# Norms of the queries as rows in a gated cross-attention and local-attention kernel on Trainium2

## The reference, cut to what matters

```python
l2norm = lambda t: t / jnp.maximum(jnp.linalg.norm(t, axis=-1, keepdims=True), 1e-12)
q, k = l2norm(q) * qs, l2norm(k) * ksc
q = q * cos * scale + rotate_half(q) * sin * scale
k = k * cos * inv + rotate_half(k) * sin * inv
sim = jnp.einsum('bhwie,bhwje->bhwij', bq, bk2) * QK_SCALE
sim = jnp.where(mask, -jnp.finfo(sim.dtype).max, sim)
attn = jax.nn.softmax(sim, -1)
out = jnp.einsum('bhwij,bhwje->bhwie', attn, bv2)
```

## Time and profile before

| | |
|---|---|
| Median of 3 runs | 1986.11 us (1985.73 to 1987.9) |
| The profiled execution, own time | 1993.02 us |
| its span, first to last instruction | 1991.2 us |
| TensorE busy | 1858.3 us (93%) |
| VectorE busy | 1589.7 us (80%) |
| ScalarE busy | 1045.7 us (53%) |
| GpSimd busy | 903.9 us (45%) |
| mean granted TensorE clock | 0.970 |

### The profile page before, as it was taken

The page is one execution under the profiler, slowest core; times in us unless marked ns, Lnnn a source line. Parts: engine busy times, 40 slices in busy tenths (PEclk is TensorE's granted clock), DMA queues, the critical chain, the costliest instruction groups (busy, mean ns, idle before and its releaser), DMA issues.

```text
span 1991.2 us, 84866 instructions
## 1 busy us (share of the span) xinstructions
PE 1858.3 (93%) x35408; PEld 1303.1 (65%) x35408; DVE 1589.7 (80%) x3092; ACT 1045.7 (53%) x1879; POOL 903.9 (45%) x1231
## 2 busy tenths in 40 slices
PE   6888858899999999999999999999999999999996
PEld 3444424676767777777767677776767676777674
DVE  5565557788988888888888888888889888888883
ACT  2444423455555656555555556565556555465553
POOL 1000015364554646464555546464645555464640
PEclk7898888999999999999999999999999999999997
DMA  2001006556566656566565666565665646564650
GB/s 69 10 7 64 0 3 100 83 80 102 74 122 109 94 82 94 117 95 108 78 104 72 122 109 94 82 93 117 93 110 76 106 71 124 104 95 83 91 91 22
DMA packets 73332, 166.87 MB, mean 84 GB/s; under 512 B 16592, under 2 KB 23504, under 8 KB 72400
## 3 DMA queue, kind: packets, MB, share of 16 engines
q0 software_dynamic: 36864, 100.71, 37.9%
q1 hardware_dynamic: 36432, 65.68, 12.7%
HBM read 20.57 MB, written 1.05 MB: 11 GB/s over the span
## 4 chain that ended last, share of the span: by engine, by line
PE 69%; DVE 9%; issue 7%; DMA 2%; ACT 0%; DVEq 0%; POOL 0%; POOLq 0%; ACTq 0%
PE ps L997 14%; PE ps L1033 8%; PE ps L1087 7%; PE ps L1107 6%; PE ps L1057 6%; PE ps L1141 5%; PE ps L1009 5%; PE ps L1070 4%; PE ps L1100 3%; DVE big L815 3%; PE ps L1131 3%; PE ps L1021 3%; DVE big L825 2%; DMA big<-big 2%; PE ps L1048 2%
## 5 line engine op out<-in xcount | busy, mean ns | idle before, releaser
L477 POOL DMA_DIRECT2D big<-big x768 | 607.0, 1497 | 62.4 <-DVE big L807 43.9
L564 ACT ACTIVATE big<-ps 128x512 f32<-128x512 f32 x384 | 228.4, 595 | 587.6 <-PE ps L997 540.0
L997 PE MATMUL ps<-big,wn_sb 128*128 128x256 f32 x1536 | 411.2, 396 | 17.5 <-issue 14.9
L815 DVE TENSOR_TENSOR big<-big,ps 128x512 f32<-128x512 f32 x384 | 249.6, 680 | 93.2 <-PE ps L1021 82.8
L997 PEld LDWEIGHTS ps<-big,wn_sb 128*128 128x128 f32 x1536 | 275.4, 192 | 69.6 <-issue 16.5
L468 POOL TENSOR_TENSOR big<-big 128x512 f32<-128x512 f32 x96 | 123.4, 1285 | 360.8 <-ACT big L581 360.8
L804 DVE TENSOR_TENSOR big<-ps,tab 128x512 f32<-128x512 f32 x384 | 262.0, 682 | 11.0 <-ACT big L564 10.9
L807 DVE TENSOR_TENSOR big<-ps,tab 128x512 f32<-128x512 f32 x384 | 259.0, 674 | 0.0
L1141 PE MATMUL ps<-big,wo_sb 128*128 128x256 f32 x768 | 214.5, 382 | 0.0
L443 POOL COPY big<-xs 64x256 f32 x144 | 79.2, 550 | 263.5 <-DVE xs L843 257.6
L1033 PE MATMUL ps<-wn_sb,big 128*64 128x512 f32 x768 | 182.0, 611 | 0.7 <-DVE big L807 0.7
(11 more groups left out here) (146 smaller groups left out, 2917.1 us busy)
## 6 DMA issues: line engine op xcount, KB each, us to landing
big<-big POOLq DMA_DIRECT2D x768, 128.0 KB, 5.0
big<-big SPq DMA_DIRECT2D x96, 256.0 KB
big<-big SPq DMA_DIRECT2D x96, 192.0 KB
wn_sb<-in_wn SPq DMA_DIRECT2D x6, 1024.0 KB, 10.0
wn_sb<-in_wn SPq DMA_DIRECT2D x6, 512.0 KB, 6.1
wo_sb<-in_wo SPq DMA_DIRECT2D x6, 512.0 KB, 4.0
w_sb<-in_w SPq DMA_DIRECT2D x6, 341.0 KB, 3.0
w_sb<-in_w SPq DMA_DIRECT2D x6, 192.0 KB, 3.3
```

The source lines that it names most:

```text
L477: eng.dma_start(rot[to:to + 32, at:at + 4, :], src[32 * r:32 * r + 32], accum_op=ALU.add).then_inc(added[i], 16)
L564: eng.activation(sq[:, two, :], ps[:, i % 2, :].rearrange("p (a t) -> p a t", a=2), ACT.Square).then_inc(sq_d, 1)
L815: eng.tensor_tensor(hat[:, two, :], rot[:, two, :], ps[:, i % 2, :].rearrange("p (a t) -> p a t", a=2), ALU.mult).then_inc(hat_d, 1)
L997: mm = eng.matmul(ps[:, k % 2, a * T:a * T + T], wn_sb[:, u * P:u * P + P], sT, start=True, stop=True)
```

## The change

The queries are no longer normalized ahead of the scores. `rot` holds them as they are (with the factor 256 of the spreads put into the rotary tables), and the scores read queries from `rot` and keys from `hat`, which is half as large. The queries' reciprocal norms, made for all heads in n_r, are turned by two transposes (Q0, `turn_norms`) so that tokens lie on partitions, copied to SBUF by ScalarE (q0), and a new VectorE step M multiplies them into the scores on their way out of PSUM into `pr_`. X and D then work on `pr_` in SBUF. R and H are left for the keys alone, four each. Since `rot` is read by the scores, c0 and c4 of the next round wait for S0 and S1; S1 and the weighing steps wait for M where they waited for D. The four plans are new. N3 to N6 stay as they are. POOL_PLAN is unchanged.

```diff
@@ -57,7 +57,7 @@
 ...
     other = np.arange(P) ^ 32
-    rot = np.stack([8.0 * both(cq), 8.0 * both(sq)[other], both(ck), both(sk)[other]], 1).astype(f)
+    rot = np.stack([2048.0 * both(cq), 2048.0 * both(sq)[other], both(ck), both(sk)[other]], 1).astype(f)
     q, k = np.arange(WIN)[:, None], np.arange(KW)[None, :]
@@ -180,7 +180,7 @@
 ...
         rot = view(UNITS * T, UNITS, T)
-        hat = view(UNITS * T, UNITS, T)
+        hat = view(PAIRS * T, PAIRS, T)
         pr_ = view(2 * 2 * 512, 2, 8, 2 * KW)
@@ -203,6 +203,7 @@
 ...
         top = sb("top", [P, 2, 2, 8])
+        rq = sb("rq", [P, NT, P])
         den = sb("den", [P, 2, 2 * 8])
@@ -237,6 +238,7 @@
 ...
                    "wo_d", "x_d", "w_go", "s_go", "vf_free", "y2_d", "den_h", "den_s"))
+        rq_t, rq_d, mul_d = sem("rq_t"), sem("rq_d"), sem("mul_d")
         chain, nchain, nmid = sem("chain"), sem("nchain"), sem("nmid")
@@ -258,7 +260,7 @@
         ORDER = [*range(0, 4), *range(8, 12), *range(4, 8), *range(12, 16)]
-        HATS = [i // 2 + PAIRS // 2 * (i % 2) for i in range(PAIRS)]
+        HATS = [PAIRS // 2 + i for i in range(PAIRS // 2)]
@@ -269,13 +271,13 @@
         PE_PLAN = [(x_[0], int(x_[1:])) for x_ in """
-            S0 F1 k0 k1 S1 k2 F2 T0 k3 T1 k4 g1 W0 W1 k5 T2 k6 T3 F4 k7 U0 U1 g3 W2 W3 V0 V1 V2 V3 U2 O0 O1 F5
-            R0 O2 O3 R1 R2 U3 O4 R3 R4 O5 F6 R5 O6 R6 O7 F7 R7""".split()]
+            S0 k0 k1 F1 S1 k2 k3 F2 T0 g1 k4 T1 k5 W0 W1 k6 k7 T2 T3 g3 W2 W3 V0 V1 V2 V3 U0 Q0 U1 F4 O0 O1 U2
+            U3 O2 R0 F5 O3 O4 O5 F6 O6 O7 R1 R2 F7 R3""".split()]
         ACT_PLAN = [(x_[0], int(x_[1:])) for x_ in """
-            s0 s1 x0 F1 s2 F2 s3 t0 t1 s4 x1 F3 s5 t2 s6 t3 s7 u0 n0 v0 v1 F4 v2 u1 v3 u2 F5 u3""".split()]
+            s0 s1 F1 s2 x0 s3 F2 s4 t0 t1 s5 x1 s6 s7 t2 t3 n0 v0 v1 v2 F3 q0 u0 u1 F4 u2 u3 F5 v3""".split()]
         DVE_PLAN = [(x_[0], int(x_[1:])) for x_ in """
-            X0 X1 D0 D1 c0 d0 c1 X2 d1 D2 c2 d2 X3 f0 D3 f1 c3 f2 d3 c4 f3 d4 Z0 c5 d5 Y0 c6 d6 n0 c7 Z1 d7 Y1
-            N1 N2 N3 N4 N5 N6 H0 F5 H1 H2 H3 H4 F6 H5 e0 H6 F7 H7""".split()]
+            M0 M1 X0 X1 c0 d0 D0 c1 d1 D1 M2 M3 c2 d2 c3 d3 X2 X3 D2 c4 d4 c5 D3 d5 Z0 c6 Y0 n0 d6 c7 d7 f0 N1
+            N2 f1 f2 f3 N3 Z1 Y1 N4 N5 N6 H0 F5 F6 H1 e0 F7 H2 H3""".split()]
         POOL_PLAN = [(x_[0], int(x_[1:])) for x_ in """
@@ -555,7 +557,7 @@
 ...
             def body(b, it, l, A, Bh, F, first):
-                for kind, i in share(ACT_PLAN, A, Bh, F, "snv", "xtu", "F"):
+                for kind, i in share(ACT_PLAN, A, Bh, F, "snqv", "xtu", "F"):
           if kind == "s":
@@ -579,6 +581,11 @@
 ...
               eng.activation(chunk, chunk, ACT.Exp).then_inc(ex_d, 1)
+          if kind == "q":
+              eng.wait_ge(rq_t, it + 1)
+              if Bh:
+                  eng.wait_ge(mul_d, it * 4)
+              eng.activation(rq[:, :, :].rearrange("p n d -> p (n d)"), ps[:, 2, 0:T], ACT.Copy).then_inc(rq_d, 1)
           if kind == "t":
@@ -786,7 +793,7 @@
 ...
           eng.wait_ge(fvc, l if isinstance(b, int) else l + 1)
-                for kind, i in share(DVE_PLAN, A, Bh, F, "cdnNH", "XDZYe", "Ff"):
+                for kind, i in share(DVE_PLAN, A, Bh, F, "cdnNH", "MXDZYe", "Ff"):
           if kind == "n":
@@ -800,6 +807,8 @@
 ...
               eng.wait_ge(sq_d, it * PAIRS + (i + 1))
+          if kind == "c" and Bh and i in (0, 4):
+              eng.wait_ge(sc_d, it * 2 + (i // 4 - 1))
           if kind == "c":
@@ -808,22 +817,30 @@
 ...
               two = slice(2 * HATS[i], 2 * HATS[i] + 2)
-              eng.wait_ge(rb, it * PAIRS + (i + 1))
+              eng.wait_ge(rb, it * 4 + (i + 1))
               eng.wait_ge(added[ORDER.index(two.start) // 4], it * 64 + 64)
-              if Bh and i % 4 == 0:
-                  eng.wait_ge(sc_d, it * 2 + (i // 4 - 1))
-              eng.tensor_tensor(hat[:, two, :], rot[:, two, :], ps[:, i % 2, :].rearrange("p (a t) -> p a t", a=2),
+              if Bh and i % 2 == 0:
+                  eng.wait_ge(sc_d, it * 2 + (i // 2 - 1))
+              eng.tensor_tensor(hat[:, 2 * i:2 * i + 2, :], rot[:, two, :], ps[:, i % 2, :].rearrange("p (a t) -> p a t", a=2),
                                 ALU.mult).then_inc(hat_d, 1)
+          if kind in "MXD":
+              c, r = divmod(i, 2)
+              rows = pr_[:, c, :, KW * r:KW * r + KW]
+          if kind == "M":
+
+              eng.wait_ge(sc_d, it * 2 + (c - 1))
+              if i == 0:
+                  eng.wait_ge(rq_d, it)
+              norms = rq.rearrange("p t (q m) -> p q t m", m=32)[:, :, :, 2 * c + r:2 * c + r + 1]
+              eng.tensor_tensor(rows.rearrange("p (q t) k -> p q t k", t=NT),
+                                ps[:, 5 + r, :].rearrange("p (q t k) -> p q t k", t=NT, k=KW),
+                                norms.to_broadcast((P, 4, NT, KW)), ALU.mult).then_inc(mul_d, 1)
           if kind == "X":
-              c, r = divmod(i, 2)
-              eng.wait_ge(sc_d, it * 2 + (c - 1))
-              eng.tensor_reduce(top[:, c, r, :], ps[:, 5 + r, :].rearrange("p (g k) -> p g k", g=8), AX.X,
-                                ALU.max).then_inc(max_d, 1)
+              eng.wait_ge(mul_d, it * 4 + (i + 1 - 4))
+              eng.tensor_reduce(top[:, c, r, :], rows, AX.X, ALU.max).then_inc(max_d, 1)
           if kind == "D":
-              c, r = divmod(i, 2)
               eng.wait_ge(max_d, it * 4 + (i + 1 - 4))
-              eng.tensor_tensor(pr_[:, c, :, KW * r:KW * r + KW], ps[:, 5 + r, :].rearrange("p (g k) -> p g k", g=8),
-                                top[:, c, r, :].rearrange("p (g k) -> p g k", k=1).to_broadcast((P, 8, KW)),
+              eng.tensor_tensor(rows, rows, top[:, c, r, :].rearrange("p (g k) -> p g k", k=1).to_broadcast((P, 8, KW)),
                                 ALU.subtract).then_inc(sub_d, 1)
@@ -989,7 +1006,7 @@
 ...
           if k < 2 and Bh:
-              eng.wait_ge(hat_d, it * PAIRS + (k - 1))
+              eng.wait_ge(hat_d, it * 4 + (k - 1))
           if k >= 2:
@@ -1001,7 +1018,7 @@
 ...
           if g == 1 and Bh:
-              eng.wait_ge(ss_d, it)
+              eng.wait_ge(rq_d, it)
               eng.wait_ge(x_d, it - 1 + FREE)
@@ -1016,10 +1033,16 @@
 ...
           else:
-              eng.wait_ge(hat_d, it * PAIRS + (n - 1))
+              eng.wait_ge(hat_d, it * 4 + (n - 1))
           for a in range(2):
 ...
           mm.then_inc(rb, 1)
+
+                def turn_norms(_):
+          eng.wait_ge(nchain, it * 4 + 2)
+          for n in range(NT):
+              mm = eng.transpose(ps[:, 2, n * P:n * P + P], n_r[:, n * P:n * P + P], ident)
+          mm.then_inc(rq_t, 1)
                 def values(j):
@@ -1037,10 +1060,12 @@
 ...
               eng.wait_ge(on_d, it * 4 + (FREE - 4))
-              eng.wait_ge(hat_d, it * PAIRS - 4)
+              eng.wait_ge(hat_d, it * 4 - 2)
+              eng.wait_ge(added[0], it * 64)
           else:
-              eng.wait_ge(sub_d, it * 4 + (2 - 4))
-              eng.wait_ge(hat_d, it * PAIRS)
+              eng.wait_ge(mul_d, it * 4 + (2 - 4))
+              eng.wait_ge(hat_d, it * 4)
+              eng.wait_ge(added[2], it * 64)
           eng.sem_inc(s_go, 1)
@@ -1055,7 +1080,7 @@
 ...
                       mm = eng.matmul(ps[WIN * w:WIN * w + WIN, 5 + r, KW * g + skip:KW * g + KW],
-                                      hat[rows, p, at:at + WIN], hat[rows, PAIRS + p, at - WIN + skip:at + WIN],
+                                      rot[rows, p, at:at + WIN], hat[rows, p, at - WIN + skip:at + WIN],
                                       start=False, stop=False, skip_group_check=True)
@@ -1073,7 +1098,7 @@
 ...
           if q == 0:
-              eng.wait_ge(sub_d, it * 4)
+              eng.wait_ge(mul_d, it * 4)
               eng.wait_ge(vev, it * 4)
@@ -1136,15 +1161,15 @@
 ...
               if A:
-                  eng.wait_ge(ss_d, it + 1)
+                  eng.wait_ge(rq_d, it + 1)
           eng.wait_ge(oev, it * 4 + (p // 2 + 1 - 4))
 ...
                 steps = {"k": project, "g": head_sums, "V": values, "R": spread, "S": score, "T": turn_weights,
-               "W": weigh, "U": turn_outputs, "O": project_out, "F": ffn}
-                for kind, i in share(PE_PLAN, A, Bh, F, "kgRV", "STWUO", "F"):
+               "Q": turn_norms, "W": weigh, "U": turn_outputs, "O": project_out, "F": ffn}
+                for kind, i in share(PE_PLAN, A, Bh, F, "kgQRV", "STWUO", "F"):
           steps[kind](i)
```

## The result

The changed kernel takes 2024.59 us, median of 4 runs (2023.63 to 2025.69), against 1987.01 (1985.73 to 1990.15) for the kernel before: 1.0175 times as long, 95% interval 1.0162 to 1.0188. The prediction on record was 2026.

The account below looks back on a forecast made before the run. VectorE's string of steps was to bound the first half, TensorE the second: 20.65 + 14.18 = 34.83 us a round against 34.00, 39 us over 47 rounds added to 1986.1, about 2026 us; range 1982 to 2055.

Parts of the forecast that it names:

- The first half: First score step S0 to value projections V0: 20.65 us against 20.62, bound by VectorE's steps up to Y0, 2.1 us longer.
- Y0 hold W2: End of first half: Y0 begins at 17.9, ends at 19.15; W2, writing the banks Y0 reads, begins at 19.2.
- the sum: Whole round: 20.65 + 14.18 = 34.83 us against 34.00, 0.83 more; 39 us in 47 full rounds.
- The second half: Value projections V0 to the next score step S0: TensorE is the bound, 14.18 us against 13.37.
- the stall at R4: TensorE, second of two spreads in a row, second half: its stall goes since spreads lie apart, 0.33 us less.
- F5 is held by the Gelu: TensorE's FFN step, second half: reached at 28.75, waits for Gelu ending at 28.9, 0.1 us in the reckoning.
- TensorE as the bound throughout: Rival: only TensorE's own work counts, 0.85 us less a round, 1946 us; chance 0.14.
- No change: Rival: X and D out of SBUF cost 0.50 us, M no more; round 34.0, 1986 us; chance 0.08.
- The clock: Rival: TensorE idles more and its clock falls to 0.95, up to 1.6 us more a round, 2100 us; chance 0.04.
- The late GpSimd DMAs: GpSimd's accumulating DMAs stay hidden with 2 us of cover; rival of a new wait, 2087 us, chance 0.06.
- Z0's sum: GpSimd's first sum; it meeting VectorE's D2 is part of the new-wait rival, 1.3 us more a round, chance 0.06.
- D's second SBUF input: VectorE's D could block with GpSimd steps reading SBUF; by the walk D and GpSimd's sums never meet, no term.

Follow-up runs that it names:

- more_first: Changed kernel plus one useless VectorE step (0.60 us) between X3 and D2, in the first half of the round; 2053.4 us, 1.0317 of the kernel before.
- more_second: Changed kernel plus one useless VectorE step (0.60 us) between N6 and H0, in the second half; 2023.0 us, 1.0164 of the kernel before.
- narrow_m: Changed kernel with the four M steps multiplying only 64 of 512 columns, so computing something else; 1981.4 us, 0.9952 of the kernel before.
- c6_behind_y0: Changed kernel with VectorE's step c6, and its wait for a square, put behind Y0; 2021.5 us, 1.0158 of the kernel before.
- new_sums_old_order: Changed computation (M, Q0, q0, four R and H) put into the old kernel's order of work; 2107.6 us, 1.0579 of the kernel before.

## Why the prediction was right

**The first half.** Reckoned against measured, from S0: k3 7.2 and 7.34, T0 8.95 and 9.10, k7 16.27 and 16.31, the second exponential 15.7 and 15.69, c6 17.3 and 17.26, Y0 17.9 and 17.87, W2 19.2 and 19.25, V0 20.65 and 20.69. The claim that the work taken out of TensorE's first half buys nothing since VectorE's string is the bound is shown by more_first (0.58 of 0.60 on the path) and more_second (nothing). It is the bound by a little only: narrow_m gains 0.83 for 1.8 us before the squares hold it.

**One link was wrong.** The prediction had Y0 hold W2. c6_behind_y0 shows that d5, through k7, T2, T3 and g3, holds it as well: Y0 0.9 us earlier changed nothing. So one of the prediction's own signs, TensorE waiting for Y0 ahead of W2, is missing from the trace. The two strings end within 0.1 us of each other, so the sum did not suffer; that they do was luck.

**The second half.** 14.18 reckoned, 14.35 measured, with the parts as they were named: U0, U1, F4 and Q0 in, four R out, the stall at R4 gone (TensorE waited 1.1 us in all for H ahead of R, where it had been 13.6). F5 is held by the Gelu, as reckoned: it starts 28.92 behind S0, with the Gelu reckoned out at 28.9. By the starts of TensorE's steps the 0.17 lies in the FFN: F5 takes 0.93 and F6 0.97 to their successors, where they took 0.86 and 0.87 in the kernel before. What makes them longer was not tried.

**The sum.** The round grew by 1.04, not 0.83; 47 times that is 49 us, and the median grew by 37.6. So the total of 2026 was hit within 1.4 us partly by luck: errors cancel. What I had left out is at the ends, and the traces show it: the first S0 of the layers comes at 311.66 us where it came at 317.13 (a first round with four R and H and not eight, one behind the other, which may be why), the first two rounds together lose 6.7 us less against steady ones (the second takes 38.5 and not 41.65), the later rounds at the start of a layer 1.5 less, and from the last S0 to the end it is 52.7 and not 55.7 us. Together that is 16.7 us off the 49, and the spans of the two profiled executions do differ by 32.2. The rest is in the choice of executions: the profiled one of before lay 6.0 us above its median, that of the changed kernel 0.6.

**The rivals.** TensorE as the bound throughout fell with more_first. No change fell: X and D cost the same out of SBUF (0.60, means of 0.676 and 0.682 us). The clock did not matter (0.979 over the run against 0.970 before, and 1.00 in the steady round shown). The late GpSimd DMAs stayed hidden, as the 4.6 us of waits show, and Z0's sum met no D.

**D's second SBUF input.** D's mean of 0.682 is that of before, so nothing met, as the walk had it. N6, which had 0.67 in the earlier trace rows, has 0.48 at 1045.65 although the record of GpSimd's copies (1043.59 for 4.33) covers it. Those copies stand behind twelve DMA issues that end at 1047.06, and from there to the end of their record it is 0.86 us, what such a pair takes elsewhere (0.85 at 1053.38), so the record may be mostly waiting. Over the run the trace is clear on when N6 is long: above 0.6 us in 44 of 48 rounds before, in none of 48 in the changed kernel, and in 44 of 48 again in new_sums_old_order, where N6 and the copies start together as they did before (both at 1046.42). So its length goes with the order of work and not with the new sums. Whether it is the copies themselves that N6 meets was not tested alone.

**What M and the rest cost.** The narrow M takes 0.83 off the round, so of the 1.04 over 34.00, 0.83 goes with M's width and 0.21 with everything else together: the order, Q0, the spreads gone, and what is left of M. That is a price in this order alone.

## What to carry to other kernels

Work saved on the busiest engine was worth nothing here in the half where the second busiest had the string. So walk a steady round with the engine orders written out, half by half, and ask of each step which engine reaches it last. When a change moves a step's input (here D's, from PSUM to SBUF), look again at which engine should run the step; here that turned a loss into a gain (33.69 a round against 35.04, and against 34.00 before the change). And in an in-order queue the place of a step counts as much as its cost: two steps behind four DMA issues cost 1.42 us a round.

## What the runs showed that I had not expected

- Twelve accumulating DMA issues in a row take 9.50 us of GpSimd, 0.79 each as before. The copies behind them are recorded with 4.33 us for two, where it was 1.38. No one waited for them here.
- The first score step takes 1.55 us for its products where the second takes 1.44, and k0 starts 1.82 behind S0, where F1 stood at 1.60 before. In new_sums_old_order, with F1 behind S0 again, both are back at 1.44 and 1.60. The trace puts 0.19 us of wait ahead of k0's weights down to VectorE's H (L824), of which H2 ends 1.11 and H3 1.70 behind S0; what makes the products themselves longer was not tried.
- A 512-column subtraction on GpSimd with both inputs in SBUF takes 1.02 us, against 0.68 on VectorE and 1.28 for GpSimd's own sum of two strided halves of the same size.
